# Edge attention on a graph: SyncE fetches the rows of one step in 64 by single DMAs at row numbers in registers

## The chip, the cores and the metric

The kernel runs on one core of one Trainium2 chip. The metric is the device time of an execution in microseconds. A profile is one execution, taken apart by the hardware profiler; its span runs from the first to the last instruction.

## The reference

There are 12500 nodes with 128 features and 412500 edges (200000 drawn, their reverses, and a loop at each node). For each edge a score is computed from both its ends; the scores are normalized over the edges of a source node, weighted messages are summed there, and the result goes through a residual and a layer norm.

```python
q = (X @ Wq)[src]                       # 64 values
k = (X @ Wk)[dst]
e = tanh(q + k)
scores = e @ Wphi
exp_scores = exp(scores - max(scores))
denom = segment_sum(exp_scores, src)
alpha = exp_scores / (denom[src] + 1e-9)
msg = alpha[:, None] * ((X @ Wy_w + Wy_b)[dst] + e @ We)
out = segment_sum(msg, src)
return layernorm(x + out)
```

## The kernel before

The program sorts the edges by blocks of 128 source nodes, then walks over the sorted list, and at the end works on the nodes. A plan and a table come first: row r + 1 of `table`, in DRAM, holds the 64 values of k and the 128 features of node r (192 f32, 768 bytes). The sort leaves `sorted_list` in DRAM; one record is an integer with the table's row number above 8 bits and the source node's place in its block in the low 8.

The main part takes the list in tiles of 128 edges, four tiles a step (QUAD), four steps a chunk. There are at most 836 steps; 806 are certain and the rest runs behind branches until the tiles in use are done, here after 822 steps. Each engine has its own written-out order, and semaphores hold the engines together:

- GpSimd (`gpsimd_steps`) gathers the table's rows of a step by four indirect DMAs (L1283), one for each tile, into `gathered`, a ring of nine places (RING). It reuses a place when TensorE has summed the step nine before (semaphore `totalled`).
- One step in 16 (`ahead`, steps 8, 24, ..., 40 of them) is skipped there: its rows were gathered during the sort and lie in order in DRAM, and SyncE loads them in one DMA (L1265).
- SyncE (`sync_steps`) loads for each chunk the sources' places within their blocks, spread over all partitions, into one of two buffers (L1259, `src_in_block_rows`). It waits for VectorE to have made the one-hots of two chunks earlier.
- VectorE makes the one-hots of a chunk (L1353), and in step s adds up the query parts of step s - 1 beside the gathered rows (L1369, two reductions), adds the keys (L1373), computes the scores of step s - 2 (L1382, L1384), and adds the sums of step s - 4 to the blocks (L1406).
- ScalarE takes tanh (L1328) and makes weighted one-hots by exp (L1338, L1346).
- TensorE multiplies one-hots by the queries (L1306) for step s and weighted one-hots by the gathered rows (L1317) for step s - 3.

TensorE and VectorE load 16 registers with block offsets in each chunk (L1230). Before the main part each engine loads two single registers and computes with one (L1422 to L1425). L224 and L227 are loads and stores of one row at the start, L1153 sets the last column of all places of the ring to one.

Of the kernel before, what the change touches and what calls it, by code (L numbers as in the profile page):

```python
# [4 lines left out]
PARTS = 128  # L5
COLS = 64
UNIT = 16
QUAD = 4
# [25 lines left out]
def gnn_program(nc, x, src, dst, Wq, Wk, Wphi, Wy_w, Wy_b, We, out):  # L34
# [12 lines left out]
    ROW = A + D  # L47
# [54 lines left out]
    with ctx:  # L102
# [4 lines left out]
        identf = sb(ctx, "identity_f32", [PARTS, PARTS], f32)  # L107
        identb = sb(ctx, "identity_bf16", [PARTS, PARTS], bf16)
        before = sb(ctx, "before", [PARTS, PARTS], bf16)
        before_far = sb(ctx, "before_far", [PARTS, PARTS], bf16)  # L110
        ones = sb(ctx, "ones", [PARTS, PARTS], bf16)
        first_two = sb(ctx, "ones_in_rows_0_and_1", [PARTS, PARTS], bf16)
        wkq = sb(ctx, "wk_wq", [D, 2 * A], f32)
# [23 lines left out]

        sort, early = ExitStack(), ExitStack()
        blk = sb(sort, "edge_block", [PARTS, NT], bf16)
        rec_hi = sb(sort, "record_high", [PARTS, NT], f16)  # L140
# [31 lines left out]
        list_zeroed, table_stored = sem("list_zeroed"), sem("table_rows_stored")  # L172
        rows_made, vector_line = sem("rows_made"), sem("vector_line")
        block_high_int, high_block_made = sem("block_then_high_int"), sem("high_then_block_made")
# [58 lines left out]
        def gpsimd_early(e):  # L233
            e.iota(row1[:, :], [[1, PARTS]], base=1, channel_multiplier=0, allow_small_or_imprecise_dtypes=True).then_inc(iotas_made, 1)
            e.iota(part[:, :], [[0, 1]], base=1, channel_multiplier=1, allow_small_or_imprecise_dtypes=True).then_inc(iotas_made, 1)
            e.memset(zeros[:, :], 0).then_inc(iotas_made, 1)
            e.iota(rowt[:, :, :], [[1, max(NBH, NBL)], [0, TPG]], base=0, channel_multiplier=0,
                   allow_small_or_imprecise_dtypes=True).then_inc(rows_made, 1)
# [9 lines left out]
        def vector_early(e, line):  # L248
# [39 lines left out]
            for g in range(STEPS):  # L288
                if g < NG:
                    T, a = g_tiles[g], g * TPG  # L290
                    if g == 0:
                        e.wait_ge(rows_made, 1)
# [309 lines left out]
        def vector_plan(e, line):  # L602
# [53 lines left out]

            e.wait_ge(iotas_made, 10)
            for i in range(XSTEPS):
# [431 lines left out]
        def ahead(q):  # L1090

            return q % AHEAD_EVERY == AHEAD_AT and q // AHEAD_EVERY < AHEAD_STEPS

        def tile_of(q):
# [90 lines left out]
        gathered = [sem(f"gathered_{i}") for i in range(RING)]  # L1185
        lows_loaded = [sem(f"src_in_block_rows_loaded_{i}") for i in range(LOB)]
        ahead_loaded, sums_cleared = sem("rows_ahead_loaded"), sem("sums_cleared")
# [8 lines left out]
        leave = {k: sem(f"pass_next_{k}") for k in ENGINES if k != "sync"}  # L1196
        pass_sems = [*gathered, *lows_loaded, ahead_loaded, sums_cleared, distances_made, onehots_T_made, query_summed, queried, added_qk, tanh_made,
                     times_phi, scored, scores_shifted, weighted, totalled, accumulated, row_max, core_max, shift_made, *steps_over.values()]
# [10 lines left out]
        def landed_upto(n):  # L1209

            return sum(16 * QUAD * (not ahead(k)) for k in range(n % RING, n + 1, RING))
# [39 lines left out]

        def sync_steps(e, first, end, limit):
# [39 lines left out]
        def tensor_steps(e, regs, first, end, limit):  # L1292
            for step in range(first, end):
# [16 lines left out]
                if 0 <= q < limit:  # L1310
                    r = q % RING
                    e.wait_ge(weighted, q + 1)
                    if q >= 2:
                        e.wait_ge(accumulated, (q - 1) * QUAD)
                    for j in range(QUAD):
                        o = j % 2 * SUMS
                        made = e.matmul(SM[q % 2 * 2 + j // 2][:, o:o + SUMS], ohw[:, q % 3, j, :], slot[:, r, j, A:SLOT], start=True, stop=True)  # L1317
                    made.then_inc(totalled, 1)

        def scalar_steps(e, first, end, limit):  # L1320
            if first == 0:
                e.activation(sums[:, CLEAR:NB * SUMS], part[:, :].to_broadcast([PARTS, NB * SUMS - CLEAR]), ACT.Copy, scale=0.0).then_inc(sums_cleared, 1)
            for step in range(first, end):
                q = step - 1
                if 0 <= q < limit:
                    r = q % RING
                    e.wait_ge(added_qk, q + 1)
                    e.activation(slot[:, r, :, ROW:ROW + A], slot[:, r, :, ROW:ROW + A], ACT.Tanh).then_inc(tanh_made, 1)  # L1328
# [26 lines left out]
        def vector_steps(e, regs, first, end, limit):  # L1355
# [4 lines left out]
            for step in range(first, end):  # L1360
# [3 lines left out]
                if 0 <= q < limit:  # L1364
                    r = q % RING
                    e.wait_ge(queried, q + 1)
# [8 lines left out]
                if 0 <= q < limit:  # L1375
                    r, c = q % RING, q // QUADS_PER_CHUNK
                    e.wait_ge(tanh_made, q + 1)
# [63 lines left out]
        out_stored = [sem(f"out_stored_{i}") for i in range(FO)]  # L1441
        x_again_padded, eps_set, sums_turned, sumsT_made, numerators = sem("x_again_padded"), sem("eps_set"), sem("sums_turned"), sem("sumsT_made"), sem("numerators")
        residuals, stats_made, means_made, deviations = sem("residuals"), sem("stats_made"), sem("means_made"), sem("deviations")
# [14 lines left out]
        def sync_final(e):  # L1458
            for step in range(NF + FLAG):
                i = step  # L1460
                if i < NF:
# [3 lines left out]
                    if whole < n:  # L1465
                        e.wait_ge(x_again_padded, 1)
                    if whole:
# [70 lines left out]
        def vector_final(e, line):  # L1538
# [5 lines left out]
            for step in range(NF + FLAG):  # L1544
                i = step
                if i < NF and f_split(i)[2] < f_split(i)[1]:
                    if i >= FX:
                        e.wait_ge(residuals, i - FX + 1)
                    e.memset(fx[:, i % FX, f_split(i)[2], :], 0.0).then_inc(x_again_padded, 1)
                i = step - 3  # L1550
# [46 lines left out]
        def _(e):  # L1597
# [7 lines left out]
            fence(e, "sync", 4)  # L1605
            rounds, used_tiles = pass_count(e, "sync")
            with e.Fori(0, rounds):
                in_parts(e, lambda first, end, limit: sync_steps(e, first, end, limit), used_tiles, None)
                over(e, "sync")
# [109 lines left out]
```

## Time and profile before

| | |
|---|---|
| median of three runs | 5815.66 us (5815.23 to 5815.95) |
| the profiled execution, span | 5233.9 us |
| the median less that span | 581.8 us |
| main part, first to last step | about 1196 to 5138 us of the span |
| busy, share of the span | TensorE 65%, VectorE 80%, ScalarE 70%, GpSimd 72% |
| mean granted TensorE clock | 0.797 |
| instructions in the span | 83795 |

The time of the profiled execution itself is recorded as its span alone; what lies outside the first and the last instruction is the difference to the timed runs. Issuing a DMA, register instructions and waits are not counted as busy. "Issue" as the end of an idle time means that the engine waited for nothing that the profile shows. The engine names of the rows are PE (TensorE), DVE (VectorE), ACT (ScalarE), POOL (GpSimd) and SP (SyncE); a "q" behind one is its sequencer.

### The profile page before, as it was taken

How to read it: one execution, taken by the hardware profiler on the slowest of the kernel's cores; microseconds unless marked ns; L12 is line 12 of the kernel's file. 1: busy time of each engine (PE TensorE's matmuls, PEld its weight loads, DVE VectorE, ACT ScalarE, POOL GpSimd, SP SyncE). 2: the span in 40 equal slices, each digit the busy share in tenths (PEclk: the TensorE clock that was granted, in tenths of full speed). 3: DMA queues.
4: the chain of work that ended last, by engine and by line, in shares of the span. 5: the costliest groups of instructions: out<-in, count | busy, mean ns of one | idle time of the engine just before them, and what ended most of it. 6: DMA issues, size and time to landing. Idle time of an engine off the chain costs nothing. (4 is left out here: it accounts for less than half of the span.)

```text
span 5233.9 us, 83795 instructions
## 1 busy us (share of the span) xinstructions
PE 3420.2 (65%) x19333; PEld 2674.0 (51%) x19333; DVE 4209.8 (80%) x9868; ACT 3654.0 (70%) x14079; POOL 3747.1 (72%) x3677
## 2 busy tenths in 40 slices
PE   7799999965555655556656555655655565555557
PEld 6666665644444444444444444444544444444446
DVE  6799999978877777777777777777777777777777
ACT  3699999966766666666666666666666666666665
POOL 1046888777777777777777777777777777777775
PEclk9899999987777777777777777777777767776768
DMA  3201111124343443344333434434444333333334
GB/s 94 75 9 32 51 45 50 47 66 129 113 112 110 112 112 110 108 112 113 109 112 113 109 108 113 112 109 113 113 110 111 108 106 107 103 106 103 104 102 118
DMA packets 337130, 509.17 MB, mean 97 GB/s; under 512 B 118108, under 2 KB 251518, under 8 KB 336382
## 3 DMA queue, kind: packets, MB, share of 16 engines
q0 software_dynamic: 165888, 325.74, 24.0%
q1 hardware_dynamic: 164830, 175.98, 10.6%
q8 instruction: 175, 2.87, 0.2%
q14 instruction: 317, 2.60, 0.2%
q10 hardware_dynamic: 5920, 1.97, 0.2%
HBM read 471.72 MB, written 36.85 MB: 97 GB/s over the span
## 5 line engine op out<-in xcount | busy, mean ns | idle before, releaser
L1283 POOL DMA_INDIRECT gathered<-table,dst_rows x3108 | 2995.4, 964 | 946.8 <-issue 932.4
L1317 PE MATMUL bank<-gathered,weighted_onehots 128*128 128x193 f32 x6576 | 1832.0, 440 | 1435.8 <-DVE block_sums L1406 1433.7
L1317 PEld LDWEIGHTS bank<-gathered,weighted_onehots 128*128 128x128 f32 x6576 | 1510.3, 257 | 1634.6 <-issue 990.7
L1406 DVE TENSOR_TENSOR block_sums<-block_sums,bank 128x193 f32 x3288 | 1165.9, 355 | 524.6 <-issue 155.1
L1369 DVE TENSOR_REDUCE gathered<-bank 128x128 f32<-128x384 f32 x1644 | 837.5, 552 | 292.9 <-DMA gathered<-table,dst_rows 283.9
L1338 ACT ACTIVATE weighted_onehots<-src_distances,score_less_shift 128x128 f32<-128x128 bf16 x3288 | 1049.8, 390 | 26.8
L1328 ACT ACTIVATE gathered<-gathered 128x256 f32<-128x256 f32 x822 | 345.5, 420 | 1016.8 <-DVE gathered L1373 1016.8
L1346 ACT ACTIVATE src_distances<-row_to,src_in_block 128x128 bf16<-128x128 f32 x3288 | 1037.1, 386 | 0.0
L985 ACT ACTIVATE places_past_far<-bank,stat 128x98 bf16<-128x98 f32 x2727 | 892.1, 1217 | 7.0 <-PE bank L1010 5.9
L985 ACT ACTIVATION_READ_ACCUMULATOR places_past_far<-bank,stat 128x1 f32 x2727 | 888.1, 1077 | 0.0
L1306 PE MATMUL bank<-q_parts,src_onehots_T 128*128 x3288 | 607.5, 314 | 196.0 <-DVE gathered L1373 159.6
L1306 PEld LDWEIGHTS bank<-q_parts,src_onehots_T 128*128 128x128 bf16 x3288 | 396.1, 121 | 437.3 <-issue 386.2
L1033 POOL DMA_INDIRECT sorted_list<-sorted_groups,unit_destinations x248 | 372.3, 1501 | 281.2 <-DVE sorted_groups L949 215.3
L1332 ACT ACTIVATE score_less_shift<-scores,stat 128x4 f32<-128x4 f32 x822 | 244.4, 297 | 307.7 <-DVE scores L1384 305.5
L1010 PE MATMUL bank<-block_onehots,before_far 128*128 128x392 bf16 x806 | 410.1, 509 | 0.0
L1017 PE MATMUL bank<-col_records,row_onehots 128*128 128x128 f16 x3223 | 402.7, 298 | 6.9 <-DVE col_records L922 6.9
L1017 PEld LDWEIGHTS bank<-col_records,row_onehots 128*128 128x128 bf16 x3223 | 375.2, 117 | 48.0 <-issue 27.7
L1373 DVE TENSOR_TENSOR gathered<-gathered 128x256 f32<-128x256 f32 x822 | 354.7, 432 | 28.2
L1384 DVE TENSOR_REDUCE scores<-e_times_phi 128x4 f32<-128x256 f32 x822 | 345.3, 420 | 28.1
L1382 DVE TENSOR_TENSOR e_times_phi<-gathered,phi 128x256 f32<-128x256 f32 x822 | 344.5, 419 | 0.8
L1009 PE MATMUL bank<-base_parts_flat,ones_in_rows_and 128*128 128x392 bf16 x806 | 286.1, 355 | 84.6 <-DVE places L932 64.7
L1046 POOL DMA_INDIRECT rows_ahead<-table,dst_rows_ahead x160 | 274.8, 1718 | 48.8 <-issue 48.8
(240 smaller groups left out, 2552.1 us busy)
## 6 DMA issues: line engine op xcount, KB each, us to landing
src_in_block_rows<-src_in_block_list SPq DMA_DIRECT2D x166, 512.0 KB
gathered<-table,dst_rows POOLq DMA_INDIRECT x3108
rows_gathered_ahead<-rows_ahead SPq DMA_DIRECT2D x40, 384.0 KB
src_in_block_rows<-src_in_block_list SPq DMA_DIRECT2D x40, 384.0 KB
gathered<-rows_gathered_ahead SPq DMA_DIRECT2D x40, 384.0 KB, 3.9
table<-in_x SPq DMA_DIRECT2D x4, 1562.5 KB
x_in<-in_x SPq DMA_DIRECT2D x24, 256.0 KB, 3.1
x_again<-in_x SPq DMA_DIRECT2D x48, 128.0 KB, 2.7
```

What stands on the lines that cost most here:

```text
L985: made = e.activation(past_far[:, k % 3, j, :], PL[b % len(PL)][:, j * NB:(j + 1) * NB], ACT.Relu, bias=NEAR, accum_out=pos[:, g % 2, t0 + ...
L1010: e.matmul(o, before_far[:, :], hot[:, g % 2, c, h0 // PB, :, 0:mt].rearrange("p b t -> p t b"), start=False, stop=True).then_inc(placed, 1)
L1017: made = e.matmul(O[:, 0:2 * COLS], hotr[:, k, t // PB, :, t % PB], recc[:, k, :, t // PB, :, t % PB], start=c + t == 0, stop=c * SORT_CHU ...
L1033: e.indirect_dma_start(slist, bass.IndirectOffsetOnAxis(ap=dest[:, o:o + 1].bitcast(u32), axis=0), sortd[:, g, j * UNIT:(j + 1) * UNIT], N ...
L1283: e.indirect_dma_start(slot[:, r, j, 0:ROW], None, table, bass.IndirectOffsetOnAxis(ap=rows.bitcast(u32), axis=0)).then_inc(gathered[r], 16)
L1306: made = e.matmul(QK[q % 2][j // 2][:, j % 2 * 3 * A:(j % 2 + 1) * 3 * A], ohT[:, c % 2, o:o + PARTS], q3[:, bass.ds(b, 3 * A)], start=Tru ...
L1317: made = e.matmul(SM[q % 2 * 2 + j // 2][:, o:o + SUMS], ohw[:, q % 3, j, :], slot[:, r, j, A:SLOT], start=True, stop=True)
L1338: made = e.activation(ohw[:, q % 3, j, :], off[:, q % 2, j, :], ACT.Exp, bias=shifted[:, q % 3, j:j + 1], scale=-APART)
L1346: made = e.activation(off[:, q % 2, j, :], row1[:, :], ACT.Abs, bias=lo[:, t:t + 1], scale=-1.0)
L1369: made = e.tensor_reduce(slot[:, r, 2 * h:2 * h + 2, ROW:ROW + A], QK[q % 2][h][:, 0:6 * A].rearrange("p (j s f) -> p j f s", s=3, f=A), A ...
L1373: e.tensor_tensor(slot[:, r, :, ROW:ROW + A], slot[:, r, :, ROW:ROW + A], slot[:, r, :, 0:A], ALU.add).then_inc(added_qk, 1)
L1406: e.tensor_tensor(sums[:, bass.ds(b, SUMS)], sums[:, bass.ds(b, SUMS)], SM[q % 2 * 2 + j // 2][:, o:o + SUMS], ALU.add).then_inc(accumulat ...
```

## The change

Steps 60, 124, 188, ... (one in 64) are "fetched". GpSimd skips them. SyncE fetches their 512 rows with one DMA for each row, at a row number that it holds in a register, 32 rows behind each chunk's load: it loads 32 records of the sorted list from DRAM into 32 registers, shifts each by 8 bits and issues a DMA of 768 bytes from that row of the table to one partition. The 16 batches of a step begin with the load of the chunk 14 before its own, and end with that of the chunk after it; so nearly every chunk has one batch. The rows go into a tenth place beside the ring. The first batch waits until TensorE has summed the fetched step before (64 earlier); a step is awaited by one of five semaphores that count 16 for each row. The steps behind the branches keep the rule, and at the end SyncE waits for all that it issued, which includes batches of step 828 that is not reached.

To make room, five constant tiles (`identity_bf16`, `before`, `before_far`, `ones`, `ones_in_rows_0_and_1`) now live only as long as the sort, and two semaphores are merged with others (`rows_made` into `iotas_made`, `x_again_padded` into `x_padded`).

```diff
+        FETCH_EVERY, FETCH_AT, FETCH_ROWS = 64, 60, 32
+        FETCHED = RING
+        FETCHES = QUAD * PARTS // FETCH_ROWS
+        FETCH_AHEAD, FETCH_SEMS = 14, 5
-        slot = sb(lists, "gathered", [PARTS, RING, QUAD, SLOT], f32)
+        slot = sb(lists, "gathered", [PARTS, RING + 1, QUAD, SLOT], f32)
+        def fetched(q):
+            return q % FETCH_EVERY == FETCH_AT and q < NQD
+        def place_of(q):
+            return FETCHED if fetched(q) else q % RING
...
         def wait_for_rows(e, q):
             if ahead(q):
                 e.wait_ge(ahead_loaded, 16 * (q // AHEAD_EVERY + 1))
+            elif fetched(q):
+                e.wait_ge(rows_fetched[q // FETCH_EVERY % FETCH_SEMS], 16 * QUAD * PARTS * (q // FETCH_EVERY // FETCH_SEMS + 1))
...
+        def fetch_at(c):
+            return [(f, c - (f // QUADS_PER_CHUNK - FETCH_AHEAD)) for f in fetch_steps if 0 <= c - (f // QUADS_PER_CHUNK - FETCH_AHEAD) < FETCHES]
+        def fetch_rows(e, regs, f, m):
+            t, p = tile_of(f) + m * FETCH_ROWS // PARTS, m * FETCH_ROWS % PARTS
+            if m == 0 and f >= FETCH_EVERY + FETCH_AT:
+                e.wait_ge(totalled, f - FETCH_EVERY + 1)
+            e.load(regs, slist[t * PARTS + p:t * PARTS + p + FETCH_ROWS, :].rearrange("(a n) u -> a (n u)", a=1))
+            for i in range(FETCH_ROWS):
+                row = nc.s_assert_within(e.snap(regs[i], min_val=0, max_val=(N << 8) + 255) >> 8, 0, N, skip_runtime_bounds_check_because="records hold a row of the table and 8 bits")
+                e.dma_start(slot[p + i:p + i + 1, FETCHED, m * FETCH_ROWS // PARTS, 0:ROW], table[bass.ds(row, 1), :]).then_inc(rows_fetched[f // FETCH_EVERY % FETCH_SEMS], 16)
...
         def sync_steps(e, regs, first, end, limit):
...
+                for f, m in fetch_at(c):
+                    fetch_rows(e, regs, f, m)
...
         def gpsimd_steps(e, first, end, limit):
             for q in range(first, min(end, limit)):
-                if ahead(q):
+                if ahead(q) or fetched(q):
                     continue
```

In the steps of TensorE, ScalarE and VectorE, `r = q % RING` becomes `r = place_of(q)`.

## Rows read from the trace of the kernel before

**Rows 1.** The page: busy time of each engine, share of the span, and instructions.
```profile
PE 3420.2 (65%) x19333; PEld 2674.0 (51%) x19333; DVE 4209.8 (80%) x9868; ACT 3654.0 (70%) x14079; POOL 3747.1 (72%) x3677
```

**Rows 2.** The page's costliest groups: busy, mean ns | idle before, ended by.
```profile
L1283 POOL DMA_INDIRECT gathered<-table,dst_rows x3108 | 2995.4, 964 | 946.8 <-issue 932.4
...
L1369 DVE TENSOR_REDUCE gathered<-bank 128x128 f32<-128x384 f32 x1644 | 837.5, 552 | 292.9 <-DMA gathered<-table,dst_rows 283.9
```

**Rows 3.** Two windows of the main part: busy time, clock, DMA share, GB/s.
```profile
1196.00:4270.00 3074.00, 1823.27 (x7790) 1481.62 (x7789) 2421.13 (x6160) 2052.02 (x6491) 2336.50 (x2422) 0.76 0.40 111
4270.00:5138.00 868.00, 511.61 (x2056) 414.06 (x2056) 643.47 (x1625) 542.35 (x1716) 654.71 (x683) 0.72 0.37 103
```

**Rows 4.** Order of time after a step stored ahead: start, length, engine, line.
```profile
2718.64 0.82 DVE L1353 TENSOR_SCALAR src_onehots_T<-src_in_block_rows,partition_number_from 128x2048 bf16<-128x2048 bf16 x1
...
2719.49 56.12 SPq L1259 DMA_DIRECT2D src_in_block_rows<-src_in_block_list  x5
...
2730.72 1.02 DVE L1369 TENSOR_REDUCE gathered<-bank 128x128 f32<-128x384 f32 x2 [0.79 <-DMA gathered<-table,dst_rows]
...
2735.72 1.01 DVE L1369 TENSOR_REDUCE gathered<-bank 128x128 f32<-128x384 f32 x2
...
2738.18 0.75 DVE L1353 TENSOR_SCALAR src_onehots_T<-src_in_block_rows,partition_number_from 128x2048 bf16<-128x2048 bf16 x1
...
2740.57 1.01 DVE L1369 TENSOR_REDUCE gathered<-bank 128x128 f32<-128x384 f32 x2
...
2744.48 1.01 DVE L1369 TENSOR_REDUCE gathered<-bank 128x128 f32<-128x384 f32 x2
...
2744.70 1.86 PE L1317 MATMUL bank<-gathered,weighted_onehots 128*128 128x193 f32 x8 [0.35 <-DVE block_sums L1406]
...
2748.38 1.01 DVE L1369 TENSOR_REDUCE gathered<-bank 128x128 f32<-128x384 f32 x2
...
2753.31 1.01 DVE L1369 TENSOR_REDUCE gathered<-bank 128x128 f32<-128x384 f32 x2
...
2755.70 0.76 DVE L1353 TENSOR_SCALAR src_onehots_T<-src_in_block_rows,partition_number_from 128x2048 bf16<-128x2048 bf16 x1
...
2758.10 1.01 DVE L1369 TENSOR_REDUCE gathered<-bank 128x128 f32<-128x384 f32 x2
```

**Rows 5.** Waits of SyncE: us in total, times, longest.
```profile
SPq L1259 <- DVE src_onehots_T L1353: 3631.4, 204, 31.1
...
SPq L1265 <- PE bank L1317: 153.1, 39, 4.5
```

**Rows 6.** Issues on SyncE by source line: ns minimum/median/maximum; landing in us.
```profile
L1259 SPq DMA_DIRECT2D src_in_block_rows<-src_in_block_list x246: 319/320/885, 1185.8 to 5082.6; - x123
...
L1265 SPq DMA_DIRECT2D gathered<-rows_gathered_ahead x40: 523/524/599, 1198.9 to 4151.2; - x40
...
DMA to landing us min/median/max: 3.3/3.9/5.7
...
L227 SPq DMA_DIRECT2D table<-table_row x1: 251/251/251, 15.2 to 15.2; - x1
...
L224 SPq DMA_DIRECT2D we_bias<-in_L_gnn_Wy_b x1: 437/437/437, 5.5 to 5.5; - x1
```

**Rows 7.** Order of time on SyncE, two neighbouring issues.
```profile
5.45 0.44 SPq L224 DMA_DIRECT2D we_bias<-in_L_gnn_Wy_b  x1
5.93 0.33 SPq L225 DMA_DIRECT2D phi<-in_L_gnn_Wphi  x1
```

**Rows 8.** Register instructions by source line: ns minimum/median/maximum.
```profile
L1230 DVEq TENSOR_LOAD <-tile_blocks x206: 1095/1123/1326, 1204.7 to 5144.9; - x103
...
L1424 SPq TENSOR_LOAD <-tiles_used x1: 285/285/285, 1185.3 to 1185.3; - x1
...
L1425 SPq FUSED_REGOPS  x1: 52/52/52, 1185.7 to 1185.7; - x1
```

**Rows 9.** The setting of the places' last column, by source line.
```profile
L1153 DVE MEMSET gathered<- x1: 88/88/88, 1181.5 to 1181.5; 128x36 f32 x1
```

More of the change, by code:

```diff
@@ L107, in gnn_program @@
         identf = sb(ctx, "identity_f32", [PARTS, PARTS], f32)
[L108 to L112, printed above, removed]
         wkq = sb(ctx, "wk_wq", [D, 2 * A], f32)
@@ L138, in gnn_program @@
         sort, early = ExitStack(), ExitStack()
+        identb = sb(sort, "identity_bf16", [PARTS, PARTS], bf16)
+        before = sb(sort, "before", [PARTS, PARTS], bf16)
+        before_far = sb(sort, "before_far", [PARTS, PARTS], bf16)
+        ones = sb(sort, "ones", [PARTS, PARTS], bf16)
+        first_two = sb(sort, "ones_in_rows_0_and_1", [PARTS, PARTS], bf16)
         blk = sb(sort, "edge_block", [PARTS, NT], bf16)
@@ L172, in gnn_program @@
         list_zeroed, table_stored = sem("list_zeroed"), sem("table_rows_stored")
-        rows_made, vector_line = sem("rows_made"), sem("vector_line")
+        vector_line = sem("vector_line")
         block_high_int, high_block_made = sem("block_then_high_int"), sem("high_then_block_made")
@@ L291, in vector_early @@
                     if g == 0:
-                        e.wait_ge(rows_made, 1)
+                        e.wait_ge(iotas_made, 4)
                         e.wait_ge(high_block_made, 1)
@@ L655, in vector_plan @@
             e.tensor_copy(steph[0:NE, :, :].rearrange("p g s -> p s g"), stepi[0:NE, 1:3, :]).then_inc(step_parts, 1)
-            e.wait_ge(iotas_made, 10)
+            e.wait_ge(iotas_made, 11)
             for i in range(XSTEPS):
@@ L1092, in ahead @@
             return q % AHEAD_EVERY == AHEAD_AT and q // AHEAD_EVERY < AHEAD_STEPS
+        def fetched(q):
+            return q % FETCH_EVERY == FETCH_AT and q < NQD
+        def place_of(q):
+            return FETCHED if fetched(q) else q % RING
+        assert not any(fetched(q) and (ahead(q) or q % QUADS_PER_CHUNK or q < OPENING) for q in range(NQD))
         def tile_of(q):
@@ L1185, in gnn_program @@
         gathered = [sem(f"gathered_{i}") for i in range(RING)]
+        fetch_steps = [q for q in range(NQD) if fetched(q)]
+        rows_fetched = [sem(f"rows_fetched_{i}") for i in range(FETCH_SEMS)]
         lows_loaded = [sem(f"src_in_block_rows_loaded_{i}") for i in range(LOB)]
@@ L1196, in gnn_program @@
         leave = {k: sem(f"pass_next_{k}") for k in ENGINES if k != "sync"}
-        pass_sems = [*gathered, *lows_loaded, ahead_loaded, sums_cleared, distances_made, onehots_T_made, query_summed, queried, added_qk, tanh_made,
+        pass_sems = [*gathered, *rows_fetched, *lows_loaded, ahead_loaded, sums_cleared, distances_made, onehots_T_made, query_summed, queried, added_qk, tanh_made,
                      times_phi, scored, scores_shifted, weighted, totalled, accumulated, row_max, core_max, shift_made, *steps_over.values()]
@@ L1209, in landed_upto @@
         def landed_upto(n):
-            return sum(16 * QUAD * (not ahead(k)) for k in range(n % RING, n + 1, RING))
+            return sum(16 * QUAD * (not ahead(k) and not fetched(k)) for k in range(n % RING, n + 1, RING))
         def wait_for_rows(e, q):
@@ L1250, in in_parts, with sync_landed, sync_steps @@
             more(SURE)
-        def sync_steps(e, first, end, limit):
+        def fetch_at(c):
[8 more added lines that the diff above has]
+                e.dma_start(slot[p + i:p + i + 1, FETCHED, m * FETCH_ROWS // PARTS, 0:ROW], table[bass.ds(row, 1), :]).then_inc(rows_fetched[f // FETCH_EVERY % FETCH_SEMS], 16)
+        def sync_landed(e, end):
+            issued = [0] * FETCH_SEMS
+            for q in range(0, end, QUADS_PER_CHUNK):
+                for f, m in fetch_at(q // QUADS_PER_CHUNK):
+                    issued[f // FETCH_EVERY % FETCH_SEMS] += 16 * FETCH_ROWS
+            for i in range(FETCH_SEMS):
+                if issued[i]:
+                    e.wait_ge(rows_fetched[i], issued[i])
+        def sync_steps(e, regs, first, end, limit):
             for q in range(-(-first // QUADS_PER_CHUNK) * QUADS_PER_CHUNK, min(end, limit), QUADS_PER_CHUNK):
@@ L1310, in tensor_steps @@
                 if 0 <= q < limit:
-                    r = q % RING
+                    r = place_of(q)
                     e.wait_ge(weighted, q + 1)
@@ L1325, in scalar_steps @@
                 if 0 <= q < limit:
-                    r = q % RING
+                    r = place_of(q)
                     e.wait_ge(added_qk, q + 1)
@@ L1364, in vector_steps @@
                 if 0 <= q < limit:
-                    r = q % RING
+                    r = place_of(q)
                     e.wait_ge(queried, q + 1)
@@ L1375, in vector_steps @@
                 if 0 <= q < limit:
-                    r, c = q % RING, q // QUADS_PER_CHUNK
+                    r, c = place_of(q), q // QUADS_PER_CHUNK
                     e.wait_ge(tanh_made, q + 1)
@@ L1465, in sync_final @@
                     if whole < n:
-                        e.wait_ge(x_again_padded, 1)
+                        e.wait_ge(x_padded, 2)
                     if whole:
@@ L1548, in vector_final @@
                         e.wait_ge(residuals, i - FX + 1)
-                    e.memset(fx[:, i % FX, f_split(i)[2], :], 0.0).then_inc(x_again_padded, 1)
+                    e.memset(fx[:, i % FX, f_split(i)[2], :], 0.0).then_inc(x_padded, 1)
                 i = step - 3
@@ L1606, in _ @@
             rounds, used_tiles = pass_count(e, "sync")
+            regs = [e.alloc_register(f"sync_row{i}") for i in range(FETCH_ROWS)]
             with e.Fori(0, rounds):
-                in_parts(e, lambda first, end, limit: sync_steps(e, first, end, limit), used_tiles, None)
+                in_parts(e, lambda first, end, limit: sync_steps(e, regs, first, end, limit), used_tiles, lambda end: sync_landed(e, end))
                 over(e, "sync")
```

4 lines of the change are left out of this document (2 added, 2 removed).

## The prediction

> **What bounds the kernel now.** I began with the busy line and the costliest groups of the page. Three quarters of the span is one place, the steps of the main part, so I asked for the busy time of that stretch in two windows, then for its order of time after a step whose rows were stored ahead, and last for SyncE: its waits, the length of its DMA issues and of register instructions.
>
> The busy line does not name the bound: VectorE has 80% and GpSimd 72% [rows 1]. The groups do. The gathers of L1283 are 3108; each is busy 964 ns, and nearly all the idle time before them (932.4 of 946.8 us) ends in "issue", so GpSimd waited for nobody [rows 2]. One gather takes (2995.4 + 946.8) / 3108 = 1.268 us, a step of four 5.07 us. VectorE's reductions of L1369 waited 283.9 us for gathered rows in the same time [rows 2]: GpSimd is behind, the others wait for it. There are 822 steps (1644 reductions, two a step), 40 of them loaded from rows stored ahead. As long as one step in 16 is such a step, 64 steps take 60 x 5.07 = 304.4 us; after step 640 they take 64 x 5.07 = 324.7 us.
>
> The windows agree: in the two stretches the DMA engines are busy 0.40 and 0.37 of the time, and VectorE, the busiest engine, 2421 of 3074 and 643 of 868 us, so none of them is full [rows 3].
>
> SyncE does almost nothing here. It waits 3631.4 us for VectorE's one-hots, 204 times [rows 5], which is the free time that the change wants to use.
>
> **What the change takes from the bound.** Steps 60, 124, ... 764 are twelve of the 822. Each loses its four gathers: 12 x 5.07 = 60.9 us off GpSimd's chain. Nothing on GpSimd replaces them. 64 steps would take 299.4 us (319.7 after step 640).
>
> Whether the other engines can follow is seen after a step from stored rows, where GpSimd has a lead. The reduction at 2730.72 waited for its gather; those at 2740.57, 2744.48, 2748.38, 2753.31 and 2758.10 did not, and four steps took 17.53 us, 4.38 each [rows 4]. The new mean is 299.4 / 64 = 4.68 us. The 283.9 us of waiting [rows 2] also exceed 60.9.
>
> **What it adds: SyncE's chunk.** A chunk is four steps, some 19 us, and each one from the second on now carries 32 row fetches. Per chunk SyncE has:
>
> - What it does today. In four chunks, five issues of L1259 at 320 ns and one of L1265 at 524 ns [rows 6], each with a gap of 0.04 us (one issue ends at 5.45 + 0.44, the next starts at 5.93 [rows 7]): 2.4 us, or 0.6 us a chunk.
> - One load of 32 registers from the list in DRAM. Loading 16 registers from SBUF takes 1.123 us, one register 0.285 us [rows 8], so 0.056 us for each further one: 0.285 + 31 x 0.056 = 2.0 us. That is the lower bound, as no row reads registers from DRAM. The upper one is 32 single loads, 9.1 us. I take 2.0, because one instruction with many registers is the nearest row.
> - 32 times a shift and an address in registers, and a DMA of one row. A fused register instruction takes 52 ns [rows 8], with the gap 0.09 us; I assume one per row. The DMA: the two one-row issues of this trace took 251 ns (after a wait) and 437 ns (behind a 64-row one) [rows 6]; the usual one of the main part takes 320. With gaps a row is 0.38, 0.45 or 0.57 us; 32 are 12.2, 14.4 or 18.1 us. I take the middle, as it is the issue that SyncE makes here.
>
> The sum is T = 0.6 + 2.0 + 14.4 = 17.0 us a chunk (14.8 to 20.8 by the row's bounds alone).
>
> The Trainium skill's page "Runtime: NRT & Kernel Launch", section "Instruction fetch mechanics", speaks against this: it gives about 200 ns for each register loaded, in bulk too. By it the load would be 6.4 us, T 21.4 and the time, by the formula below, 6411 us. The row of 16 registers shows a third of that per register [rows 8], but from SBUF; for a load from DRAM no row here agrees or disagrees.
>
> **Is 17.0 us short enough?** One place holds the fetched rows, so the first batch for step f waits until TensorE has summed step f - 64, and the sixteenth must land before step f is reduced. From reduction to sum is 2746.56 - 2735.72 = 10.8 us [rows 4]; landing takes 3.9 us by the nearest row [rows 6]. A round of 64 steps therefore takes SyncE at least 16 T + 15 us. At T = 17.0 this is 287, below 299.4, and GpSimd stays the bound. The turning point is T = 17.8 us: 0.78 us a chunk, or 24 ns a row, above my sum. That is thin.
>
> Behind that first wait stand the next chunk's source-row load and the load of stored rows. The load of a chunk goes out right behind the one-hots of two chunks earlier (2718.64, issue at 2719.49) and is used at 2755.70, 36 us later [rows 4]. The wait lasts from step f - 67 to f - 61, some 28 us, and the batch 17: the next load comes at 45 instead of 19 us, 26 late, with 36 - 4 = 32 to spare. So VectorE does not wait for it; SyncE regains 2 us with each further chunk. That SyncE is stopped here now and then is not new: L1265 waited 153.1 us in 39 cases [rows 5].
>
> **The rest** is costed at nothing. The last column of ones is set in ten places instead of nine, where nine take 88 ns [rows 9]. Merged semaphores keep the order of the same instructions, the moved constants are not read in the main part. GpSimd skips a step without an instruction. The 6,500 rows add 768 bytes each, 5 MB to 509. The end waits for SyncE's batches for a step that never comes (828); they go out in chunks 193 to 205, and SyncE's idle time hides them.
>
> **Sum.** The profiled execution has a span of 5233.9 us; 581.8 us of the median of 5815.66 lie around it, which I leave as they are. The span becomes 5173.0, the time 5815.66 - 60.9 = 5755 us. From no change, 0.2% (12 us) is about what a measurement of this kernel can tell.
>
> **Rivals.**
>
> *SyncE's issue is the bound (slower).* If one fetch costs more than 0.474 us in all (the turning point: (17.8 - 2.6) / 32), SyncE paces the rounds. Time then moves by 10 x (16 T + 15 - 304.4) + 2 x (16 T + 15 - 324.7) = 192 T - 3513 us. At 437 ns an issue, T is 20.8: +480, 6296 us. Halfway, T = 19.3: +192, 6008 us. For it speak the growth of issues that follow each other (437 ns [rows 6, 7]), a possible second register instruction (another 0.09 us), and the thin margin; against it the 251 ns of a single row [rows 6].
>
> *The register load is the bound (slower).* If a register from DRAM costs as much as a load of its own, T = 0.6 + 9.1 + 14.4 = 24.1: +1114, 6929 us; from 2.8 us upward the load alone takes the margin. The page of the Trainium skill cited above lies between. Against it: 16 registers cost far less than 16 loads [rows 8].
>
> *The other engines cannot follow (same).* If the steps with stored rows go no faster than today's 4.76 us, only the two fetched steps past 640 gain: 10 us, 5806 us. Against it stand the 4.38 us [rows 4].
>
> **Chances.** The forecast 0.53, issue-bound 0.30, load-bound 0.12, the others can't follow 0.05. So faster 0.53, same 0.05, slower 0.42. The likeliest case alone has 5745 to 5775: the lower end is a gather at its step's full price and some quicker steps, the upper end a few late rounds. The range must reach far into the slower cases: up to 6150 us, where 192 T - 3513 = 334 and T = 20.0. Beyond lie the top of the issue's bounds (0.05) and most of the load-bound case (0.10), below 5745 some 0.03.
>
> **What would show it.** Right: L1283 x3060, the reductions' wait for gathers down by some 60 us, SyncE's chunk of load and 32 issues under 17.8 us, and its wait for one-hots (L1259) still large. Wrong: that wait near zero, VectorE waiting at L1369 for rows that SyncE fetched or at L1353 for source rows, and GpSimd idle on TensorE's sums. The single cause that would decide it is the length of one fetch: above 0.474 us, or one load above 2.8 us, the forecast falls.

## The result, and the profile after

The changed kernel takes 7343.48 us (median of four runs, 7334.15 to 7363.82), the kernel before 5815.57: a ratio of 1.262 (1.261 to 1.264). It is 1528 us slower. The forecast was 5755 us, 60.9 less than before, and its range ended at 6150. The profiled execution of the changed kernel took 7334.49 us and its span is 7332.7.

From the page: the span and three of the costliest groups (busy, mean ns | idle before, ended most by). Lines after the change are some 42 higher: L1325 is the gather, L1411 the reduction, L1395 the one-hots of a chunk.

```profile
span 7332.7 us, 103642 instructions
...
L1325 POOL DMA_INDIRECT gathered<-table,dst_rows x3060 | 2906.3, 950 | 3104.2 <-PE bank L1359 1983.5
...
L1411 DVE TENSOR_REDUCE gathered<-bank 128x128 f32<-128x384 f32 x1644 | 834.2, 550 | 858.7 <-DMA gathered<-rows_gathered_ahead 504.9
...
L1395 DVE TENSOR_SCALAR src_onehots_T<-src_in_block_rows,partition_number_from 128x2048 bf16<-128x2048 bf16 x206 | 157.4, 764 | 1549.0 <-DMA src_in_block_rows<-src_in_block_list 1540.9
```

The 48 gathers are gone, as intended, but GpSimd, which waited for nobody in [rows 2], now waits 1983.5 us for TensorE's sums. VectorE, whose one-hots waited for nothing (0.0 in the line of the kernel before that follows), waits 1540.9 us for source rows, 504.9 us for rows stored ahead and 311.9 us for fetched rows. These three are SyncE's to deliver, and TensorE's sums come late behind VectorE.

```profile
L1353 DVE TENSOR_SCALAR src_onehots_T<-src_in_block_rows,partition_number_from 128x2048 bf16<-128x2048 bf16 x206 | 157.6, 765 | 0.0
```

```profile
DVE gathered L1411 <- DMA gathered<-table: 311.9, 12, 28.5
```

SyncE's waits in the main part (us, times, longest):

```profile
SPq L1278 <- PE bank L1359: 116.3, 10, 12.1
```

That is the whole list. The 3631.4 us that SyncE waited for one-hots in [rows 5] are gone: SyncE is late at all times, and sets the pace. What it executes, by source line (count; ns minimum/median/maximum; first and last start in us):

```profile
L1278 SPq TENSOR_LOAD <-sorted_list x205: 2806/4426/6069, 1185.2 to 7221.0; - x103
L1280 SPq FUSED_REGOPS  x6560: 1/73/1407, 1191.3 to 7239.4; - x199
L1281 SPq MOVE gathered<-table x6560: 1/29/1405, 1191.5 to 7239.5; - x199
L1281 SPq DMA_DIRECT2D gathered<-table x6560: 1/228/1405, 1191.5 to 7239.5; - x199
```

205 batches lie between 1191.5 and 7239.5 us, so a chunk takes SyncE T = 6048 / 205 = 29.5 us. The forecast had 17.0. Chunk by chunk, SyncE in order of time (start, length, x how many):

```profile
2990.39 21.73 SPq L1281 DMA_DIRECT2D gathered<-table  x32
3012.17 0.36 SPq L1299 DMA_DIRECT2D src_in_block_rows<-src_in_block_list  x1
3012.59 0.56 SPq L1305 DMA_DIRECT2D gathered<-rows_gathered_ahead  x1
3018.99 22.07 SPq L1281 DMA_DIRECT2D gathered<-table  x32
3041.11 0.36 SPq L1299 DMA_DIRECT2D src_in_block_rows<-src_in_block_list  x1
3046.16 14.66 SPq L1281 DMA_DIRECT2D gathered<-table  x32
```

The same 32 fetches take 14.66 us in one chunk and 22 in others. Here is the batch of 2990.39 in two pieces, with the gathers beside it:

```profile
2987.24 0.95 POOL L1325 DMA_INDIRECT gathered<-table,dst_rows  x1 [0.30 <-issue]
2999.17 0.94 POOL L1325 DMA_INDIRECT gathered<-table,dst_rows  x1 [10.98 <-PE bank L1359]
3000.42 0.95 POOL L1325 DMA_INDIRECT gathered<-table,dst_rows  x1 [0.30 <-issue]
...
3007.92 0.95 POOL L1325 DMA_INDIRECT gathered<-table,dst_rows  x1 [0.30 <-issue]
```

```profile
2990.39 8.69 SPq L1281 DMA_DIRECT2D gathered<-table  x19
3000.64 9.86 SPq L1281 DMA_DIRECT2D gathered<-table  x6
L1281 SPq MOVE gathered<-table x19: 29/29/29, 2990.3 to 2998.8; - x19
L1281 SPq MOVE gathered<-table x6: 4/21/700, 3000.6 to 3009.8; - x6
```

While GpSimd waited, 19 rows went out in 8.7 us, a row in 0.47, every move in exactly 29 ns. While eight gathers ran, 6 rows took 9.9 us, and a move in registers could last 700 ns. In such a stretch SyncE's instructions, register ones too, start 0.70 or 1.40 us apart; I call these stops. An undisturbed row is 0.447 us (73 ns, then 29 at +0.110, then 228 at +0.170 and the next at +0.447): 14.3 us for 32.

So the 29.5 us are 0.6 for today's issues, 4.4 for the load, 14.3 for the rows and some 10 of stops (among them 116.3 / 205 = 0.6 us of the waits above).

### The profile page after: what moved, and what is told of

It reads as the page before. It is cut to its first block and busy times, and to the rows that moved or that the text cites. A ratio compares the mean times of both kernels' runs of the same rounds, so it can differ in the third digit from the quotient of the medians.

```text
span 7332.7 us, 103642 instructions
## 1 busy us (share of the span) xinstructions
PE 3352.1 (46%) x19333; PEld 2648.5 (36%) x19333; DVE 4183.7 (57%) x9868; ACT 3654.2 (50%) x14079; POOL 3656.6 (50%) x3629
## 5 line engine op out<-in xcount | busy, mean ns | idle before, releaser
L1325 POOL DMA_INDIRECT gathered<-table,dst_rows x3060 | 2906.3, 950 | 3104.2 <-PE bank L1359 1983.5
L1359 PE MATMUL bank<-gathered,weighted_onehots 128*128 128x193 f32 x6576 | 1801.3, 434 | 2910.6 <-DVE block_sums L1448 2615.7
L1411 DVE TENSOR_REDUCE gathered<-bank 128x128 f32<-128x384 f32 x1644 | 834.2, 550 | 858.7 <-DMA gathered<-rows_gathered_ahead 504.9
L1395 DVE TENSOR_SCALAR src_onehots_T<-src_in_block_rows,partition_number_from 128x2048 bf16<-128x2048 bf16 x206 | 157.4, 764 | 1549.0 <-DMA src_in_block_rows<-src_in_block_list 1540.9
L1348 PE MATMUL bank<-q_parts,src_onehots_T 128*128 x3288 | 579.2, 303 | 885.7 <-DVE gathered L1415 761.0
```

The costliest lines, as they stand in the source:

```text
L1325: e.indirect_dma_start(slot[:, r, j, 0:ROW], None, table, bass.IndirectOffsetOnAxis(ap=rows.bitcast(u32), axis=0)).then_inc(gathered[r], 16)
L1348: made = e.matmul(QK[q % 2][j // 2][:, j % 2 * 3 * A:(j % 2 + 1) * 3 * A], ohT[:, c % 2, o:o + PARTS], q3[:, bass.ds(b, 3 * A)], start=Tru ...
L1411: made = e.tensor_reduce(slot[:, r, 2 * h:2 * h + 2, ROW:ROW + A], QK[q % 2][h][:, 0:6 * A].rearrange("p (j s f) -> p j f s", s=3, f=A), A ...
```

## The experiments

Behind each run stand its median, the ratio to the kernel before that was timed beside it, and the ratio's 95% interval.

**The kernel before again.** Nothing is edited. The profile that the prediction read has a span 581.8 us under the timed median; a second profile was to show where those lie.

> The kernel before, unchanged, timed against itself. What is open is the 581.8 us between the median of before (5815.6) and the span of its profiled execution (5233.9), where the changed kernel shows a span of 7332.7 in an execution of 7334.5. If the span of a timed execution of before is some 2 us below its time, the two kernels' timed runs can be compared as they are and the profiled execution of before was a quicker one by 10%; if its span stays near 5234, 580 us lie outside of the instructions.

5818.78 us, ratio 0.9999 (0.9989 to 1.0009), and a span of 5813.5. Three of its groups, to be held against [rows 2], and then the additions (L1406) in the first trace:

```profile
span 5813.5 us, 83795 instructions
...
L1283 POOL DMA_INDIRECT gathered<-table,dst_rows x3108 | 3008.3, 968 | 1499.5 <-issue 848.3 <-remote 568.3 <-PE bank L1317 82.6
L1406 DVE TENSOR_TENSOR block_sums<-block_sums,bank 128x193 f32 x3288 | 1167.1, 355 | 1089.8 <-remote 565.6 <-issue 112.1 <-PE bank L1317 86.2
L1369 DVE TENSOR_REDUCE gathered<-bank 128x128 f32<-128x384 f32 x1644 | 834.9, 550 | 328.1 <-remote 316.1 <-issue 9.9 <-PE bank L1306 2.0
```

```profile
L1406 DVE TENSOR_TENSOR block_sums<-block_sums,bank 128x193 f32 x3288 | 1165.9, 355 | 524.6 <-issue 155.1 <-PE bank L1317 40.2 <-DVE block_sums L1406 5.3
```

The instructions last as long as before, but GpSimd idles 1499.5 us in place of 946.8, VectorE before its additions 1089.8 in place of 524.6. "Remote" is a release that the profile can't name: this trace has 29528 records of semaphore updates where the first has 81943, for the same 83795 instructions. So the 581.8 us don't lie around the steps, they are in them: 5.45 us a step from step 64 to 640 in place of 4.76. What follows is held against this pace.

In this trace GpSimd isn't behind, as it is in [rows 2]. From a step's first gather to its first reduction it is 30.5 us (median of steps 64 to 640; 7.4 in the first trace), and of GpSimd's 274 waits of over 1 us 144 end within 0.1 us of the start of VectorE's additions, as these two do:

```profile
3010.84 1.34 DVE L1406 TENSOR_TENSOR block_sums<-block_sums,bank 128x193 f32 x3 [4.64 <-remote]
3010.89 0.95 POOL L1283 DMA_INDIRECT gathered<-table,dst_rows  x1 [2.16 <-remote]
```

Both wait for TensorE's sums, GpSimd for a place in its ring.

**Fixed row numbers.** No load, no register instruction:

```diff
-            e.load(regs, slist[...])
-                row = nc.s_assert_within(e.snap(regs[i], ...) >> 8, 0, N, ...)
-                e.dma_start(slot[...], table[bass.ds(row, 1), :])...
+                row = (t * PARTS + p + i) * 37 % N
+                e.dma_start(slot[...], table[row:row + 1, :])...
```

> The changed kernel with row numbers fixed when the program is written (other rows than the list asks for): no load of registers, no register instruction, 32 one-row DMAs a chunk as before. Theory (SyncE's chunk is the bound: load 4.4, register part 0.17 and issue 0.28 us a row, and stops of about 10 us a chunk while gathers run): without stops the chunk is 0.6 + 32 x 0.28 = 9.6 us, far below 17.8, so GpSimd is the bound again and the time is 5755 us (0.990). Rival 1 (the wait for the one place and the landing of one-row DMAs make the rounds long, whatever SyncE issues): as slow as the change, above 7000 us. Rival 2 (each one-row DMA is stopped by the gathers): between, 6000 to 6800 us.

5811.67 us, 0.9989 (0.9979 to 0.9998). A DMA takes 252 ns, one follows the other in 0.295, and SyncE keeps up with the steps (it again waits for one-hots, 153.0 us). The 1528 us are gone, and yet next to nothing of the 60 us appears.

**The load as well.** Row numbers fixed except for the last of each batch:

```diff
+                row = last if i == FETCH_ROWS - 1 else (t * PARTS + p + i) * 37 % N
```

> As the run with fixed rows, but the load of 32 registers is kept and the last row of each batch uses its register. Theory: chunk 0.6 + 4.45 + 31 x 0.28 + 0.45 = 14.2 us without stops; below 17.8, so 5755 to 5800 us. If the load of registers is what the gathers stop (4.4 us instead of the 2.0 of the forecast), it is still below. Rival (the load blocks SyncE's DMA queue or is itself far longer beside full-rate gathers): above 6200 us.

5917.79 us, 1.0174 (1.015 to 1.0198). The issues of the two runs, the first with fixed rows alone, the second with the load:

```profile
L1280 SPq DMA_DIRECT2D gathered<-table x6560: 3/252/1425, 1184.6 to 5675.1; - x199
```

```profile
L1282 SPq DMA_DIRECT2D gathered<-table x6560: 1/252/1453, 1200.5 to 5800.2; - x199
```

With the load a chunk is (5800.2 - 1200.5) / 205 = 22.4 us, and SyncE sets the pace. Its undisturbed sum would be 0.6 + 3.9 + 32 x 0.295 = 14.0.

**One step in 128, 16 rows a chunk.**

```diff
-        FETCH_EVERY, FETCH_AT, FETCH_ROWS = 64, 60, 32
+        FETCH_EVERY, FETCH_AT, FETCH_ROWS = 128, 124, 16
...
-        FETCH_AHEAD, FETCH_SEMS = 14, 5
+        FETCH_AHEAD, FETCH_SEMS = 30, 5
```

> Half the rate: one step in 128 (steps 124 to 764, six of them) and 16 rows behind each chunk's load. Theory: chunk 0.6 + 2.8 + 16 x 0.45 = 10.6 us and stops of 5 to 10 us: 15 to 20 us, where a chunk of GpSimd takes 19; the time is 5785 us (0.995) if SyncE keeps up, and up to 6100 if the stops do not shrink with the rows. Rival (slot wait and landing): six rounds of 128 steps, each late by what a round of 64 is late now (some 120 us): 6500 us.

5984.31 us, 1.0286 (1.0266 to 1.0307). Half the rows, and a chunk still takes 22.7 us:

```profile
L1281 SPq DMA_DIRECT2D gathered<-table x3072: 2/228/1403, 1188.0 to 5547.2; - x192
```

Undisturbed it would be 0.6 + 2.4 + 16 x 0.447 = 10.2. The remaining 12.5 us are no less than the 10 of the changed kernel: the stops of a chunk do not shrink with SyncE's rows, and SyncE's time is not a fixed sum.

**Twelve steps without gathers, nothing in their place** (in the kernel before):

```diff
+        def skipped(q):
+            return q % 64 == 60 and not ahead(q)
...
-                if ahead(q):
+                if ahead(q) or skipped(q):
                     continue
```

> The kernel before, in which steps 60, 124, ... 764 issue no gathers and nothing else takes their place: SyncE has none of the new work, and these twelve steps work on the rows that step q - 9 left in the ring (so they use other rows than the list's). Forecast's theory, that GpSimd's gathers set the pace: 60.9 us less, 5755 us. Rival, that in the timed executions the other engines set the pace and GpSimd is ahead of them (a step's reduction starts some 26 us after its gathers are issued in the second trace of the kernel before, 2.5 us in the first): 5805 to 5820 us.

5758.56 us against 5819.68, 0.9899 (0.9883 to 0.9916): 61.1 us less, 49 to 68 by the interval. The size of the prediction's first term, 60.9, stands in the timed executions too, and the time of my rival falls. What the rival went by stands as well: GpSimd is ahead there, here too (30 us from gather to reduction). So the way by which fewer gathers shorten these executions is not the prediction's "GpSimd is behind, the others wait for it"; which it is no run here shows. GpSimd's group here, and the same in the run with fixed row numbers:

```profile
L1287 POOL DMA_INDIRECT gathered<-table,dst_rows x3060 | 2954.1, 965 | 1491.5 <-issue 840.5 <-remote 526.7 <-PE bank L1321 124.3
```

```profile
L1324 POOL DMA_INDIRECT gathered<-table,dst_rows x3060 | 2958.2, 967 | 1544.6 <-issue 844.9 <-remote 592.9 <-PE bank L1358 106.8
```

With the 6560 issues GpSimd idles 53 us longer (1544.6 against 1491.5), and the time is 53 us longer (some 37 to 67 by the two intervals).

**Gathers in one step of four** (in the kernel before; `skipped` is q >= 64 and q % 4 != 1).

> The kernel before, in which from step 64 on only steps q with q mod 4 = 1 gather their rows, and the others work on the rows that are left in the ring; nothing is added on SyncE. It asks what stretches a step from 4.8 to 5.5 us in the timed executions. If the stops come with GpSimd's gathers: the steps go at the pace of the other engines, 4.38 us, so about 1195 + 822 x 4.4 + 97 = 4910 us, up to 5100. If the stops have nothing to do with the gathers: 5.5 us a step as before, 5815 us.

4966.87 us, 0.8535 (0.8518 to 0.8552), and VectorE's idle time before its additions falls from 1089.8 to 562.3 us, near the 524.6 of the first trace. GpSimd, then the additions:

```profile
L1287 POOL DMA_INDIRECT gathered<-table,dst_rows x980 | 933.1, 952 | 2711.3 <-PE bank L1321 2434.9 <-issue 234.5 <-remote 41.9
L1410 DVE TENSOR_TENSOR block_sums<-block_sums,bank 128x193 f32 x3288 | 1163.9, 354 | 562.3 <-issue 161.4 <-remote 40.5 <-PE bank L1321 33.1
```

Steps take 4.39 us, what the prediction read as the pace of the other engines. What stretches the steps of the kernel before goes with the gathers.

**The same in the changed kernel.**

> The changed kernel, SyncE's fetches untouched, in which from step 64 on only steps q with q mod 4 = 1 gather their rows and the others work on rows left in the ring. It asks whether the 10 us of slow instructions in SyncE's chunk of 29.3 us come with the gathers. If they do: a chunk of 0.6 + 4.4 + 14.3 = 19.4 us, at most 22, so 1195 + 206 x (19.4 to 22) + 97 = 5290 to 5830 us. If SyncE is slow by itself: 29.3 us a chunk, 7340 us.

5937.49 us, 1.0203 (1.0183 to 1.0224):

```profile
L1285 SPq DMA_DIRECT2D gathered<-table x6560: 2/228/787, 1196.9 to 5850.7; - x199
```

SyncE's work is untouched and a chunk falls from 29.5 to 22.7 us. Of the 10 us of stops 3.4 are left, with a quarter of the gathers; a little more than I allowed for.

**The fetches without the load.** The 32 registers are loaded once:

```diff
+            e.load(regs, slist[0:FETCH_ROWS, :]...)
...
-            e.load(regs, slist[t * PARTS + p:...])
```

> The changed kernel without the 205 loads: the 32 registers are loaded once ahead of the steps, and every batch fetches the same 32 rows by them, with both register instructions and the DMA of each row kept (so the rows fetched are not the list's). By the sum (a chunk loses 4.4 of 29.3 us, and all the rest of it stays): 192 x 4.4 = 845 us less, 6500 us. Rival, that the loads and what is queued behind them are the greater part: 5820 to 6000 us, near the kernels whose row numbers are fixed. Second rival, that the load is hidden: 7340 us.

6971.45 us, 1.198 (1.1956 to 1.2004). A chunk takes 27.7 us:

```profile
L1280 SPq DMA_DIRECT2D gathered<-table x6560: 1/228/1404, 1198.7 to 6875.1; - x199
```

The load is worth 1.8 us of the chunk, less than the 4.4 that it lasts: the stops between the rows grow to 12.8 us when it is gone. The first theory was 470 us too low for that reason; both rivals fall.

**Register instructions alone.** The kernel before, and behind each chunk's loads (the result also enters one load's address at step 800, as a zero, here and in the run after this):

```diff
+                for i in range(96 if c else 0):
+                    e.reg_alu(regs[0], regs[1], 8, ALU.logical_shift_right)
+                    e.reg_mov(regs[1], regs[0])
```

> The kernel before, with all its gathers and no fetch; behind each chunk's loads from the second on SyncE runs 96 times a shift and a move in registers (one pair takes 0.17 us undisturbed in the trace of the changed kernel), no load, no DMA. Theory, that any instruction of SyncE is stopped while GpSimd gathers, by some 0.65 us a gather: a chunk of 0.6 + 16.3 + 16 x 0.65 = 27.3 us, so 1195 + 206 x 27.3 + 97 = 6920 us (6600 to 7100). Rival, that only the DMA issues are stopped and register instructions wait merely behind them: a chunk of 16.9 us, hidden, 5815 us.

5837.63 us, 1.0037 (1.0021 to 1.0053). The 96 pairs were joined into 28 instructions, so the load on SyncE was less than planned and the time can't decide. The trace does:

```profile
L1270 SPq FUSED_REGOPS  x2870: 4/224/1405, 1202.6 to 5708.1; - x192
```

With no fetch in the program, a register instruction of 224 ns lasts up to 1405. The 28 of a chunk took 7.1 us at best and 12.5 in the mean. A fetch is not needed for a stop.

**Fixed row numbers with a register instruction per row** (shift and move, joined into one of 84 ns; the DMA does not use it).

> The changed kernel without the loads and with fixed row numbers, but with a shift and a move in registers ahead of each row's DMA, whose result the DMA does not use (the rows are other rows than the list's). Theory, that the two register instructions of a row cost what they last and are stopped like the rest: a chunk of 0.6 + 32 x (0.295 + 0.17) + 16 x 0.7 = 26.7 us; from the step times of the timed executions a round has 349 us for 16 chunks and 12 us of waiting, so 10 x (16 x 26.7 + 12 - 349) + 2 x (16 x 26.7 + 12 - 368) = 1045: 6860 us (6650 to 7050). Rival, that the address in a register makes the DMA dear: as with fixed rows alone, 5812 to 5900 us.

**The address from one register** (`row` is made once a chunk, so only a move stands between the DMAs).

> The changed kernel without the loads, and the 32 DMAs of a chunk all take their row number from one register that is shifted once a chunk, so that no register instruction stands between them (all 32 fetch the same row). Theory, that each instruction counts and the address in a register costs the DMA nothing: a chunk of 0.6 + 32 x 0.27 + 16 x 0.5 to 0.7 = 17 to 20 us, below the 21 that a round allows: 5810 to 5850 us. Rival, that a DMA with its address in a register is what GpSimd's gathers hold up: 6900 to 7000 us, as with 32 registers.

6352.79 us, 1.0916 (1.0892 to 1.094), and 6254.79 us, 1.0748 (1.0727 to 1.0768). The first run's issues, then the second's:

```profile
L1282 SPq DMA_DIRECT2D gathered<-table x6560: 1/214/1408, 1189.4 to 6234.2; - x199
```

```profile
L1280 SPq MOVE gathered<-table x6560: 1/29/1422, 1196.3 to 6149.9; - x199
L1280 SPq DMA_DIRECT2D gathered<-table x6560: 1/225/1409, 1196.3 to 6150.0; - x199
```

Chunks of 24.6 and 24.2 us. Both times lie between my two theories: a DMA with its address in a register is no longer than one without, and one more instruction per row, of whatever kind, takes the chunk from under 21.9 to over 24 us. For the second run I had 17 to 20, as I took 0.5 to 0.7 us of stops a gather; it is about 0.9 ((24.2 - 0.6 - 32 x 0.32) / 15 gathers).

**One step in 256, 8 rows a chunk** (256, 252, 8; 62 chunks ahead).

> The changed kernel with FETCH_EVERY, FETCH_AT, FETCH_ROWS, FETCH_AHEAD = 256, 252, 8, 62: three fetched steps in place of twelve, 8 rows a chunk. SyncE's chunk is 0.6 + 1.4 + 8 x 0.45 = 5.6 us and with stops of at most 10 us still below 21, so it paces nothing. Theory, that SyncE must only stay below its chunk: 3 x 5.07 = 15 us less for GpSimd, and of the 53 us that 6560 issues with fixed rows cost the others a quarter comes back: 5800 to 5820 us. Rival, that the loads and fetches cost the other engines more than the gathers saved, as with one step in 128: 5850 to 5950 us.

5825.36 us, 1.0011 (1.0002 to 1.002): no gain, a little above what I expected and far below the rival.

**Gathers of 32 rows** (in the changed kernel, three steps in four):

```diff
+                    few = 32 if q >= 64 and q % 4 != 1 else PARTS
-                    e.indirect_dma_start(slot[:, r, j, 0:ROW], ...
+                    e.indirect_dma_start(slot[0:few, r, j, 0:ROW], ...
```

> The changed kernel, SyncE untouched, with all 3060 gathers of GpSimd, of which from step 64 on those of steps q with q mod 4 other than 1 take 32 rows in place of 128 (the other rows of the place are left from earlier steps). It asks what of a gather stops SyncE. If each gather does, whatever its size: 29.5 us a chunk as before, 1292 + 206 x 29.5 = 7340 to 7370 us. If it is the rows: 0.25 + 0.75 x 0.25 = 0.44 of them are left, so the 9.4 us of stops between a chunk's rows become 4.1: 24.2 us a chunk, 6280 us (6000 to 6400).

7514.23 us, 1.291 (1.2886 to 1.2933): no better, a little worse. The gathers and SyncE's issues, then the queue of the gathers (packets, MB, share) in the changed kernel and here:

```profile
L1326 POOL DMA_INDIRECT gathered<-table,dst_rows x3060 | 2761.9, 903 | 3420.8 <-PE bank L1360 2242.6 <-issue 843.1 <-remote 335.2
L1281 SPq DMA_DIRECT2D gathered<-table x6560: 1/228/1405, 1193.8 to 7415.4; - x199
```

```profile
q0 software_dynamic: 163584, 321.02, 16.6%
```

```profile
q0 software_dynamic: 130240, 167.37, 9.2%
```

A chunk is 30.3 us. Under half the rows are moved, and GpSimd is busy 903 ns a gather in place of 950. So it is not the rows or bytes that a gather moves that stop SyncE. But the bytes fall to a half and the packets only to four fifths: whether it is the gather as an instruction or the packets that even a small one makes, this run does not separate.

**Fixed row numbers, one step in 128.**

> As the run with fixed row numbers (no load, no register instruction), for one step in 128 with 16 rows a chunk: six steps without gathers, 3072 fetches. Theory, that with one in 64 SyncE stood just at its bound (21.9 us a chunk with its waits) and lost the gain there: now 0.6 + 16 x 0.295 + at most 12 of stops = 17.3 us, and 6 x 5.07 = 30 us are gained: 5785 to 5795 us. Rival, that each fetched row costs the other engines 53 / 6560 us wherever SyncE stands: 25 of the 30 us are lost, 5810 to 5820 us.

5817.67 us, 0.9995 (0.9986 to 1.0004). SyncE waits 1110.4 us for one-hots in this run, so it is far from its bound, and the 30 us are lost all the same:

```profile
SPq L1298 <- DVE src_onehots_T L1394: 1110.4, 94, 34.4
```

If six steps without gathers are worth 30 us, half of what twelve are, each fetched row costs the others 8 to 10 ns, an estimate from two runs: 53 us for 6560, some 29 for 3072.

## Why the prediction was wrong

*What bounds the kernel: right in size, not in its way.* Dropping twelve steps' gathers gives 61.1 us where 60.9 were worked out, and with few gathers the others go at 4.39 us a step where 4.38 was read. But "GpSimd is behind, the others wait for it" describes the first trace alone. In the second, which has the span of the timed executions, the gathers are some 30 us ahead of their use and GpSimd waits for its ring, so that the two numbers agree to 0.2 us is in part luck (the interval is 49 to 68).

*SyncE's chunk: the step that failed.* The prediction put T at 17.0 us, with bounds of 14.8 to 20.8, and the turning point at 17.8. It was 29.5. The sum left one term out, what SyncE's instructions lose beside the gathers, and mis-sized another, the load:

- The load: 2.0 forecast, 4.4 measured. The Trainium skill's page "Runtime: NRT & Kernel Launch", section "Instruction fetch mechanics", would have given 6.4 with its 200 ns a register; the trace has 4.43 / 32 = 138 ns. The row from SBUF was the wrong one to lean on.
- The 32 rows: 14.4 forecast, 14.3 undisturbed. Right in the sum, though made otherwise: two register instructions a row where I assumed one, and a DMA of 228 ns where I took 320.
- The stops: about 10 us, of which the prediction has nothing. It priced an instruction by how long it lasts on a SyncE that had been idle; no row of before has SyncE busy beside GpSimd's gathers.

With the load alone T would have been 19.4. At the pace of the profile I read (a round of 304.4 us) that is past the turning point, at the pace of the timed executions (64 x 5.45 = 348.6, so (348.6 - 15) / 16 = 20.9) it is not. The stops decide: they are the greater part of the 12.5 us between 17.0 and 29.5, and with a quarter of the gathers the chunk falls to 22.7 us.

*From T to the time: right.* Put 29.5 into 192 T - 3513 and the steps grow by 2151 us; from the span of 5233.9 to that of 7332.7 it is 2099. Where SyncE sets the pace it is simpler still: 1292 us outside the steps (1195 before, 97 behind) and 206 chunks. T is read from the same executions, so the table shows only that the steps alone grew; that SyncE sets the pace is shown by its lost waits for one-hots. (With one step in 128 the last 13 chunks have no batch.)

| run | T, us | 1292 + 206 T | measured |
|---|---|---|---|
| changed kernel | 29.5 | 7369 | 7343 |
| gathers of 32 rows | 30.3 | 7534 | 7514 |
| without the load | 27.7 | 6998 | 6971 |
| fixed rows, register instruction | 24.6 | 6360 | 6353 |
| address from one register | 24.2 | 6277 | 6255 |
| one step in 128 | 22.7 | 5968 | 5984 |
| one step in four gathered | 22.7 | 5968 | 5937 |
| fixed rows and load | 22.4 | 5906 | 5918 |

*The wait for the one place: small.* SyncE waits 116.3 us in ten cases for it, already in T.

*The 581.8 us, which I left as they are: wrong.* They were slower steps. At their pace T could have been 20.9 before the time grows, and 29.5 is beyond that too, so the sign doesn't hang on it. But they were the one sign on record that something slows the timed executions that the profile I read does not show. What slows them and SyncE's stops both shrink when gathers go; that they are the same is not shown.

*"The rest is costed at nothing": wrong by nearly as much as the gain.* Even with row numbers for free the fetches give back 53 of the 61 us. So the forecast 5755 was out of reach for SyncE's fetches at any T tried here.

*Rivals.* Issue-bound, at 0.30, is what happened, beyond the end that I gave it (T 20.8, 6296 us), since I thought of longer issues and not of stops. Load-bound holds in part: with fixed rows the load brings 106 us, and taking it away from the changed kernel 372. "The others cannot follow" gave 5806 us and is excluded by the 5758.56 us of twelve steps without gathers.

*Open.* What in a gather stops SyncE for 0.5 to 0.9 us is not settled; nor is why the first profile of before has the faster steps and the second and the timed executions do not, nor by which way a fixed-row fetch costs the others its 8 to 10 ns. One rival to all of them is the recording of the trace itself. The trace with the slower steps lacks most of its records of semaphore updates (29528 in place of 81943), and that of the changed kernel has 48807; but the first trace holds the most and has the faster steps, so their number alone does not make the stops. The Trainium skill's page "NOTIFIC — the notification-queue block", section 7.1, says that inside the block that writes such records the pipeline always pushes back rather than lose a record; whether the stops are of that kind no run here can show. With SyncE doing the fetches no version tried is faster than the kernel before by more than about 0.1%.

## What to carry to other kernels

Idle time of a queue is not room for work until its instructions have been timed beside the engines that run then: here 32 fetches took 14 us alone and 22 beside the gathers. Where work moves to another engine, write down what one period of it may last, and take the margin from the worst row, not the mean; a margin of 0.8 us in 17 was none. And hold the profile's span against the timed median first: 10% between them meant that the profile I read was of faster steps than those that are timed.

## What the runs showed of the hardware

- Beside GpSimd's indirect gathers SyncE's instructions can be 0.70 or 1.40 us apart, pure register instructions included (29 or 224 ns otherwise), 0.5 to 0.9 us in all for each gather. With a quarter of the gathers 10 us of a chunk become 3.4; with gathers of 32 rows in place of 128 they are no less.
- A load of 32 registers from DRAM takes 2.8, 4.4 and 6.1 us (minimum, median, maximum) in the changed kernel, and leaving it out brings 1.8 us a chunk.
- A DMA of one row at an address in a register issues in 228 ns, at a fixed address in 252; the register costs its own instructions, 73 and 29 ns, and not a longer DMA.
